# Two of sixteen scan states fed from SBUF with their decays in PSUM: a fused Mamba and mixture-of-experts block

## What is computed

```python
x = x + mamba_block(layernorm(x))        # inner dimension 512, 16 states
x = x + experts(layernorm(x))            # 8 experts of rank 128, the best 2 weighted

# inside mamba_block, per token t, for h of shape (512 channels, 16 states)
dA = exp(dt_t[..., None] * A)
h = h * dA + dt_t[..., None] * B_t[:, None, :] * x_t[..., None]
y = einsum('bds,bs->bd', h, C_t)
```

## Time and profile before

| | |
|---|---|
| median of 3 runs | 1298.73 us (1292.53 to 1299.13) |
| the profiled execution | 1295.5 us, its span 1293.8 us |
| PE matmul busy | 1216.8 us, 94% of the span |
| PE weight load busy | 1051.1 us, 81% |
| ACT busy | 1086.1 us, 84% |
| POOL busy | 1004.7 us, 78% |
| DVE busy | 996.5 us, 77% |
| TensorE clock granted, mean | 0.987 of full speed |
| DMA | 74.04 MB, 57 GB/s over the span |

### The profile page before, as it was taken

How to read it: one execution, slowest core, us unless ns; L and a number is a source line. 1 busy time by engine, 2 the same in 40 slices (tenths; PEclk the granted TensorE clock), 3 DMA queues, 4 the chain that set the end, 5 groups by cost and what they waited for, 6 DMA issues and landing times.

```text
span 1293.8 us, 24426 instructions
## 1 busy us (share of the span) xinstructions
PE 1216.8 (94%) x7678; PEld 1051.1 (81%) x7678; DVE 996.5 (77%) x1800; ACT 1086.1 (84%) x2656; POOL 1004.7 (78%) x760
## 2 busy tenths in 40 slices
PE   5677899999999999999999999999999999998988
PEld 3466788888888888888888888888888888898876
DVE  2597979778796977979688787978878796778733
ACT  4889999899798988989898897989889898988621
POOL 2589798888878888788888888789888877888621
PEclk8798999999999999999999999999999999999999
DMA  1411111121121111112111121202112120212010
GB/s 69 180 50 42 50 42 64 37 80 43 44 83 50 66 35 56 62 50 83 47 63 42 48 68 53 83 26 83 42 41 75 50 74 26 74 42 82 17 50 17
DMA packets 29066, 74.04 MB, mean 57 GB/s; under 512 B 3080, under 2 KB 15744, under 8 KB 26496
## 3 DMA queue, kind: packets, MB, share of 16 engines
q1 hardware_dynamic: 28928, 72.35, 16.3%
HBM read 63.56 MB, written 4.58 MB: 53 GB/s over the span
## 4 chain that ended last, share of the span: by engine, by line
PE 72%; DVE 9%; ACT 6%; issue 4%; DMA 4%; POOL 1%; DVEq 0%; ACTq 0%; SPq 0%; POOLq 0%
PE psx L1255 13%; PE psy L1274 12%; PE pst L1135 8%; PE psb L1135 7%; PE psb L1129 7%; PE psf L1129 5%; DVE h L1010 4%; PE pst L1129 4%; DMA cbc<-cw_scratch 3%; PE psf L1223 2%; ACT dA L811 2%; PE psb L1229 2%; PE psf L1162 2%; PE psf L1229 2%; DVE acc L983 2%
## 5 line engine op out<-in xcount | busy, mean ns | idle before, releaser
L1010 DVE TENSOR_TENSOR_SCAN h<-dA,state,psx 128x256 f32<-128x256 f32 x1024 | 682.5, 726 | 112.1 <-PE psx L1255 94.7
L575 POOL TENSOR_TENSOR hC<-h,bC 128x1024 f32<-128x1024 f32 x256 | 604.5, 2368 | 143.8 <-DVE h L1010 137.1
L811 ACT ACTIVATE dA<-dt,neg_a 128x256 f32<-128x256 f32 x1024 | 434.1, 499 | 0.0
L1255 PE MATMUL psx<-ident,bxT 128*128 128x128 f32 x2048 | 307.0, 276 | 21.8 <-DVE h L1010 17.3
L1255 PEld LDWEIGHTS psx<-ident,bxT 128*128 128x128 f32 x2048 | 245.5, 142 | 64.7 <-issue 25.5
L799 ACT ACTIVATE bxT<-uTs,BT 128x512 f32<-128x512 f32 x352 | 232.5, 715 | 43.6 <-PE psx L1255 42.0
L1274 PE MATMUL psy<-ident,hC 128*128 128x128 f32 x2048 | 265.7, 273 | 1.4 <-POOL hC L575 1.4
L1274 PEld LDWEIGHTS psy<-ident,hC 128*128 128x128 f32 x2048 | 233.0, 141 | 4.6 <-POOL hC L575 1.7
L559 POOL TENSOR_TENSOR bxT<-uTs,BT 128x1024 f32<-128x1024 f32 x80 | 152.0, 1900 | 13.6 <-PE psx L1255 13.5
L1135 PE MATMUL pst<-w_b_sb,cbc 128*128 128x256 f32 x480 | 110.8, 379 | 0.0
L1135 PEld LDWEIGHTS pst<-w_b_sb,cbc 128*128 128x128 f32 x480 | 90.1, 190 | 11.6
(11 more groups left out here) (173 smaller groups left out, 1672.2 us busy)
## 6 DMA issues: line engine op xcount, KB each, us to landing
bC<-bc_scratch SPq DMA_DIRECT2D x64, 512.0 KB, 3.8
cbc<-cw_scratch SPq DMA_DIRECT2D x15, 1024.0 KB, 4.7
xf<-in_x SPq DMA_DIRECT2D x16, 256.0 KB, 2.7
xk<-xn SPq DMA_DIRECT2D x16, 256.0 KB, 4.2
xb<-in_x SPq DMA_DIRECT2D x16, 256.0 KB, 4.2
out<-x SPq DMA_DIRECT2D x16, 256.0 KB, 2.2
w_in_sb<-in_w_in SPq DMA_DIRECT2D x1, 1024.0 KB, 5.2
w_ff_sb<-in_w_ff SPq DMA_DIRECT2D x1, 1024.0 KB, 5.7
```

Of the source, the lines that this page charges most:

```text
L575: nc.gpsimd.tensor_tensor(hC[:, s % RC], h[:, ring(s)], bC[:, g % RINGG, s % G:s % G + 1, :].to_broadcast([P, NJ, T]), ALU.mult).then_inc( ...
L811: last = nc.scalar.activation(dA[:, s % RA, j, :], dt[:, n[1], j, :], ACT.Exp, scale=neg_a[:, j, s:s + 1])
L1010: last = nc.vector.tensor_tensor_scan(h[:, r, j, :], dA[:, s % RA, j, :], psx[bx_bank(fill)][:, k, :], state[:, b, j, s:s + 1], ALU.mult, ...
L1255: last = nc.tensor.transpose(psx[bx_bank(fill)][:, k, j * P:(j + 1) * P], bxT[:, ring(s), j, c:c + P], ident[:, :])
```

## The change

States 14 and 15 (`DIRECT`) no longer go through `bxT` and the transposes. Their inputs u*B are formed with channels on partitions: SP copies u (`sp_l`) to a new tile `uk` in turn 2, since `sp_l` is written again in turn 6, and loads B's two rows broadcast (`bB`, 256 KB) in turn 5; for that the scratch in memory now holds B's 16 rows beside C's. GpSimd multiplies them in turns 11 and 13, the turns in which it made the two `bxT` before. The products lie in `ygt` and `sp_e`, which are free at that time.

The decays of these two states go from SBUF (`dA`) to the `psx` banks that their fills would have had: ACT writes them in four pairs, one at the start of each part of turns 13 and 14, each after the scan that last read the bank. Before, ACT wrote them in turns 11 and 12, four at a time. The scans read PSUM for the decays and SBUF for the inputs.

The residual's sum on GpSimd (`xb` = x1 + `xb`) moves from turn 11 to turn 7. To make room for `uk`, three tiles take the place of others: `low` and `cT` are parts of `nT`, `bB` is `un`; ACT and GpSimd get the waits that this needs (on fills and stores that are a turn or more earlier).

```diff
+DIRECT = (14, 15)
-POOL_STATES = (4, 6, 8, 14, 15)
+POOL_STATES = (4, 6, 8)
...
+        low = nT[:, 0, :]
+        cT = nT[0:NE, 1, :]
+        bB = un
+        def direct_inputs(s):
+            return (ygt[:, :, :].rearrange("p j (k t) -> p (j k) t", t=T), sp_e[:, :, :])[DIRECT.index(s)]
...  SP
-                    sp.dma_start(bc_scratch[m[1]], bc[S:2 * S, :]).then_inc(bc_stored, 16)
+                    sp.dma_start(bc_scratch[m[1]], bc[:, :]).then_inc(bc_stored, 16)
+                if part == 0 and s == 2:
+                    sp.wait_ge(u_done, made)
+                    sp.wait_ge(direct_done, weighed)
+                    sp.dma_start(uk[:, :, :], u[:, :, :]).then_inc(u_kept, 16)
+                if part == 0 and s == 5:
+                    sp.wait_ge(filled_in, gone)
+                    sp.dma_start(bB[:, :, :], bc_scratch[n[1]][DIRECT[0]:DIRECT[0] + ND, :].partition_broadcast(P)
+                                 ).then_inc(b_loaded, 16)
...  GpSimd
+            def weigh_direct(i, n):
+                if i == 0:
+                    pool.wait_ge(b_loaded, count(16, n, 16))
+                    pool.wait_ge(u_kept, count(16, n, 16))
+                    pool.wait_ge(filled_back, count(len(BACK_UNITS), n, 2 - len(BACK_UNITS)))
+                else:
+                    pool.wait_ge(sp_rest, count(1, n, 1 if is_last(n) else 2))
+                nc.gpsimd.tensor_tensor(direct_inputs(DIRECT[i]), uk[:, :, :],
+                                        bB[:, i:i + 1, :].to_broadcast([P, NJ, T]), ALU.mult).then_inc(direct_done, 1)
             def main(s, n, part):
+                if part == 0 and s in (11, 13):
+                    weigh_direct((11, 13).index(s), n)
...
-                if s == 11:
+                if s == 7:
                     pool.wait_ge(xb_loaded, count(16, m, 16))
                     pool.wait_ge(x1_done, count(1, m, 1))
...  ACT
-                if turn + 3 < S and not (is_first(n) and turn < -1):
+                if turn + 3 < S - ND and not (is_first(n) and turn < -1):
                     decay(turn + 3, n)
+            def decay_direct(s, part, n):
+                fill = HALVES * s + part
+                act.wait_ge(scan_done, count(FILLS, n, bx_before(fill) + 1))
+                for k in range(PAIR):
+                    j = PAIR * part + k
+                    last = nc.scalar.activation(psx[bx_bank(fill)][:, k, :], dt[:, n[1], j, :], ACT.Exp,
+                                                scale=neg_a[:, j, s:s + 1])
+                last.then_inc(direct_exp, 1)
             def main(s, n, part):
+                if s + 1 in DIRECT:
+                    decay_direct(s + 1, part, n)
...  VectorE
+                    in_psum = psx[bx_bank(fill)][:, k, :]
+                    decays, inputs = ((in_psum, direct_inputs(s)[:, j, :]) if s in DIRECT
+                                      else (dA[:, s % RA, j, :], in_psum))
+                    last = nc.vector.tensor_tensor_scan(h[:, r, j, :], decays, inputs, state[:, b, j, s:s + 1],
+                                                        ALU.mult, ALU.add)
...  PE
-                if s + 1 < S:
+                if s + 1 < S - ND:
                     fill_bx(s + 1, part, n)
```

More of the change, by code:

```diff
@@ L94, in made_at, with turned_before, turned @@
 def made_at(s):
-    return (-2, -1)[s] if s < 2 else s - 3 if s < S - 1 else S - 3
+    return (-2, -1)[s] if s < 2 else s - 3
+def turned_before(s):
+    return s - RX if s >= RX else (12, 13, 11)[s] - S
+def turned(s):
+    return HALVES * (s + 1) if s >= 0 else HALVES * (s + S + 1) - TURNED
 def ring(s):
@@ L443, in main @@
                     load_c(n, 1 + s // 4, value(count(S, n, G * (2 + s // 4 - RINGG))))
+                if part == 0 and s == 2:
+                    made, weighed = value(count(1, n, 1)), value(count(ND, n, 0))
+                    sp.wait_ge(u_done, made)
+                    sp.wait_ge(direct_done, weighed)
+                    sp.dma_start(uk[:, :, :], u[:, :, :]).then_inc(u_kept, 16)
+                if part == 0 and s == 5:
+                    gone = value(count(len(IN_UNITS), n, 1 if is_late(n) else 2 * len(IN_UNITS) + 1))
+                    sp.wait_ge(filled_in, gone)
+                    sp.dma_start(bB[:, :, :], bc_scratch[n[1]][DIRECT[0]:DIRECT[0] + ND, :].partition_broadcast(P)
+                                 ).then_inc(b_loaded, 16)
             def back(s, m):
@@ L727, in ready @@
                     act.wait_ge(filled_in, in_fill("low", m))
-                    nc.scalar.activation(low[:, :], psf[:, 0, :], ACT.Copy).then_inc(low_done, 1)
+                    act.wait_ge(filled_back, count(len(BACK_UNITS), m, -2 * len(BACK_UNITS) - 1))
+                    act.wait_ge(cw_stored, count(16, m, -48))
+                    nc.scalar.activation(low, psf[:, 0, :], ACT.Copy).then_inc(low_done, 1)
                 if s in (1, 2):
@@ L732, in ready @@
                     act.wait_ge(sp_rest, count(1, m, 0))
+                    act.wait_ge(scan_done, count(FILLS, m, -FILLS))
                     act.wait_ge(filled_dt, dt_fill(f"dt{i}", m))
@@ L796, in weigh_u @@
                     act.wait_ge(uTs_done, count(2, n, 2))
-                act.wait_ge(bx_filled, count(FILLS, n, HALVES * (ring_before(s) + 1)))
+                act.wait_ge(bx_filled, count(TURNED, n, turned(turned_before(s))))
                 for j in range(SUB):
-                    last = nc.scalar.activation(bxT[:, ring(s), j, :], uTs[:, n[1], j, :], ACT.Copy,
+                    last = nc.scalar.activation(bxT[:, s % RX, j, :], uTs[:, n[1], j, :], ACT.Copy,
                                                 scale=BT[:, n[1], j, s:s + 1])
@@ L861, in back @@
                     act.wait_ge(filled_back, back_fill("vT", m))
+                    act.wait_ge(filled_dt, count(len(DT_UNITS), m, 2 if is_late(m) else 2 * len(DT_UNITS) + 2))
+                    act.wait_ge(cw_stored, count(16, m, 0))
                     for k in range(KM):
@@ L1000, in main @@
                 b, r = n[1], ring(s)
+                fill = HALVES * s + part
                 if part == 0:
-                    dve.wait_ge(exp_done, count(S, n, s + 1))
+                    if s in DIRECT:
+                        dve.wait_ge(direct_done, count(ND, n, s - DIRECT[0] + 1))
+                    else:
+                        dve.wait_ge(exp_done, count(S - ND, n, s + 1))
                     dve.wait_ge(hc_done, count(S, n, ring_before(s) + 1))
                     dve.wait_ge(state_saved, count(S, n, ring_before(s) + 1))
-                fill = HALVES * s + part
-                dve.wait_ge(bx_filled, count(FILLS, n, fill + 1))
+                if s in DIRECT:
+                    dve.wait_ge(direct_exp, count(HALVES * ND, n, fill - TURNED + 1))
+                else:
+                    dve.wait_ge(bx_filled, count(TURNED, n, fill + 1))
                 for k in range(PAIR):
                     j = PAIR * part + k
-                    last = nc.vector.tensor_tensor_scan(h[:, r, j, :], dA[:, s % RA, j, :], psx[bx_bank(fill)][:, k, :],
-                                                        state[:, b, j, s:s + 1], ALU.mult, ALU.add)
+                    in_psum = psx[bx_bank(fill)][:, k, :]
[3 more added lines that the diff above has]
+                                                        ALU.mult, ALU.add)
                 last.then_inc(scan_done, 1)
@@ L1222, in step_sizes @@
                     j = 2 * i + k
-                    last = mm(size_bank(i, m)[:, k, :], w_dt_sb[:, j * P:(j + 1) * P], low[:, :], start=True, stop=True)
+                    last = mm(size_bank(i, m)[:, k, :], w_dt_sb[:, j * P:(j + 1) * P], low, start=True, stop=True)
                 return last
```

39 lines of the change are left out of this document (25 added, 14 removed).

## The result

| | before | after |
|---|---|---|
| median | 1296.5 us (7 runs, 1292.53 to 1299.13) | 1286.74 us (7 runs, 1281.66 to 1291.73) |
| ratio to before, 95% interval | | 0.9917 [0.9894, 0.9941] |
| the profiled execution, its span | 1295.5, 1293.8 us | 1286.74, 1284.8 us |
| TensorE clock granted, mean | 0.987 | 0.979 |

The account below looks back on a forecast made before the run. PE was taken as the bound nearly throughout mid-program (busy 74.64 of 75.18 us a step). 14 x 1.31 = 18.3 less 6 x 0.8 = 4.8 gives 13.5 off 1295.5, 1282.0; with 3.2 for the median, 1285; range 1277 to 1297.

Parts of the forecast that it names:

- Three of four fills, 1.31 a step: PE, ahead of the experts' product's end: three removed fills of 0.44 us each gain 1.31 a step.
- 14 like steps, 18.3: All steps but the first two gain 1.31 us each on PE, 18.3 us in all.
- The fourth fill becomes idle: PE behind the experts' product: it waits for DVE anyway, so idle grows from 0.33 to about 0.77, no gain.
- The first two steps, counted at 0: PE already waits for DVE there and ACT sets the pace; gain counted as 0.
- ACT's path in turns 13 and 14, slack 1.1, cost 0: Later decays start state 15's first part some 0.3 late; slack 1.1 covers it; range 0 to 0.3 a step, 0 taken.
- Scans, 0: DVE scans with PSUM and SBUF exchanged cost 0, 2.8 us at most; number and kinds of streams are the same.
- GpSimd, 0: Two products add 0.94 us a step; moving xb to turn 7's 1.56 idle makes the cost 0.
- SP and the DMAs, 0.8 in each of six steps: bB's bytes delay the store ahead of cbc by 0.8 in four middle and the last two steps, 4.8 us.
- the 16 of the forecast: DVE's waits for cbc were to grow from 11.5 to about 16 us.
- The sum: Whole kernel: 18.3 - 4.8 = 13.5 us off the profiled 1295.5, forecast 1285.
- a store at 2.7: Rival, chance 0.16: bB delays the store by 2.7, six steps give back 16.2, net 2 us, 1297.
- a ScalarE bound: Rival, chance 0.10: slow decays into PSUM make ACT the bound in turns 13 and 14; slower, 1309.
- the DMA's hiding: Rival, chance 0.20: bB's bytes do not delay the store, or slow landings fall differently; full gain 18.3, 1280.4.

Follow-up runs that it names:

- e2: Kernel before, three of four transposes left out of each of the other three fills (state 14's two, state 15's first); 1282.73 us, ratio 0.9894.
- e9: Changed kernel with ACT's four pairs of decays of states 14 and 15 making one decay each, not two; 1281.5 us, ratio 0.989.
- e4: Changed kernel with both parts of state 15 scanned on DVE ahead of the experts' sum in turn 15; 1271.83 us, ratio 0.9809.
- e5: Kernel before with only DVE's order changed: both parts of state 15 scanned ahead of the experts' sum in turn 15; 1292.43 us, ratio 0.9979.
- e10: Changed kernel with ACT's copy of the last state's columns ahead of the pair of decays in turns 13 and 14, second part; 1284.28 us, ratio 0.992.
- e6: Changed kernel with decays of states 14 and 15 back in SBUF (dA), so their scans read both operands from SBUF; 1329.0 us, ratio 1.0268.
- e8: Changed kernel with the residual's sum xb back in GpSimd's turn 11; 1284.2 us, ratio 0.9917.
- e3: Changed kernel with the load of bB moved from turn 5 to turn 6, behind the load of cbc; 1283.29 us, ratio 0.9897.
- e1: Kernel before, three of the four transposes of the last fill (state 15, second part) left out; 1296.07 us, ratio 0.9995.
- e11: e7 with e10's order on ACT; 1264.9 us, ratio 0.9761.
- e7: e4 with e3's place for the load of bB, behind cbc; 1267.31 us, ratio 0.98.

## Why the prediction came out

The forecast was 1285 and the time 1286.74. That they are so near is in part luck: the forecast started from a median of 1298.73, which seven runs put at 1296.5. Of the 13.5 us foreseen the medians show 9.8 and the two profiled executions 8.8 (9.0 of span); the ratio's interval is worth 7.6 to 13.7. The prediction is right by its main term, and smaller errors of both signs lie under it.

- **Three of four fills, 1.31 a step.** Right: 1.29 outside the loop, and e2 shows it alone. But 14 like steps, 18.3, were too many: the ordinary steps of the loop gave 0.94 to 0.98 (one 0.77), mainly as ACT reaches `sz` 0.3 too late there (e9).
- **The fourth fill becomes idle.** Right, 0.77 as said. What the prediction did not see is that this idle can be had by another order (e4), which the fill itself had barred (e5).
- **The first two steps, counted at 0.** Wrong for the second: +2.22. I argued that ACT sets the pace there, and did not draw that four pairs moved to later places then delay all behind them. e9 and e10 show it. The price is the idle together with the half clock behind it: in e10 the idle is 0.80 shorter and the step 1.63.
- **ACT's path in turns 13 and 14, slack 1.1, cost 0.** The slack was 0.70, and 0.40 a decay as taken. The first part of state 15 waited 0.84 and not 0.3. That the cost there was 0 is right (e10 moved the copy, and the step stayed). The price came behind it, ahead of L1430, where I had not looked.
- **Scans, 0.** Right, 1.39 for two. But the reason given, that number and kinds of the streams are the same, was thinner than it sounded: e6 shows that the kinds are worth over 40 us.
- **GpSimd, 0.** Right (e8).
- **SP and the DMAs, 0.8 in each of six steps.** `cbc`'s issue comes 1.0 later behind `bC`'s, and e3 takes that back, so the store does pay for bB's bytes. But the four steps of the middle paid nothing. The gate products' waits of 0.88 and 1.76 were gone after the change; they are under 0.3 in e2 and at most 0.44 in e5, where SP's queue is as before, and 0.82 and 1.04 in e1. So they vary from one execution or kernel to the next without bB; why, stays open. The last two steps lost 3.4 on their waits where 1.6 was counted, 1.4 to 2.0 of it bB's (e3), and 1.66 more by the half clock behind, which the sum did not have. DVE's waits for `cbc` in all are 11.9, and not the 16 of the forecast: the middle has none left.
- **The sum.** For the 12 steps between gate products the prediction comes to -15.7 and +3.2; the trace has -15.9, of which some 3 are in the two steps where those waits went. For the last stretch, with two steps, it comes to -2.6 and +1.6; the trace has +2.45. The second step adds 2.22 and the opening, by chance, 2.18. The rivals of a store at 2.7 and of a ScalarE bound did not come, the DMA's hiding held for the middle alone.

## What to carry to other kernels

An instruction taken out of the bound engine is worth its distance to the next start only where that engine does not then wait; where it becomes idle, look whether the removed instruction was what forced the order, and change the order next (here the second edit gave about as much as the first). Put one of a VectorE scan's two big operands into PSUM when GpSimd works beside it. Moving work later on an engine that is nearly full costs in the steps where that engine sets the pace, and an idle of PE there can be paid again in clock (in the second step 0.8 us less idle gave a step 1.63 shorter).

## What the runs showed of the hardware

- The lock in e6: 0.73 against 2.79 for a scan, and 2.37 against 2.64 for a GpSimd product.
- An ACT exponential into PSUM starts 0.40 behind the last one, as into SBUF; its own duration is 463 ns in the mean, and not 500:

```profile
L882 ACT ACTIVATE psx<-dt,neg_a 128x256 f32<-128x256 f32 x128 | 55.3, 463 | 49.7 <-DVE h L1095 49.7
```

- The same instructions ran in the opening at 0.50 in one execution and at 1.00 in another, and the first gate product moved by up to 2.5 us with it. How much of the spread between runs this is, was not measured.
- Whether half clock follows a wait of PE is not told by the wait's length alone. Behind DVE's wait for `cbc` in the last step it followed waits of PE of 1.56 (e11), 1.78 (e4) and 2.34 (changed kernel), and did not follow 0.71 (e7), 1.68 (e3) and 2.09 (e9).
- A small store's end went by what was queued ahead of it: `cbc`'s issue came 3.0 to 3.4 behind `bC`'s in ordinary steps, with the store 0.4 or 1.4 behind `bC`, and in the mean 1.0 later with the 256 KB of bB between.
